# A graph layer on one core: the first batch's inputs come and are split by chunks, its scores are finished earlier, its delta is turned by TensorE, and the groups are ordered by weight

## The chip, the cores and the metric

The kernel runs on one core of a Trainium2 chip. The metric is the time of one execution on the device in microseconds (us). Several executions are timed and their median is taken; one more execution was recorded by the profiler, and its trace is what this text reads. The engines are TensorE (PE), VectorE (DVE), ScalarE (ACT), GpSimd (POOL) and SyncE (SP), which here does nothing but issue DMAs. Each engine works through its own instructions in order.

## The reference

For each of 32 batches, with h = x[b] of 256 rows and 384 features:

```python
u = h @ h.T / sqrt(384)
p = softmax(u, axis=-1)
delta = p * adjacency
attn = delta / (delta.sum(2) + 1e-10)
h_left, h_self, h_right = (h @ W.T + b for the three weights and biases)
ctx = upper(attn) @ h_left + diag(attn) * h_self + lower(attn) @ h_right
o = relu(layernorm(ctx, eps=1e-12) * gamma + beta)
out = layernorm(x + o, eps=1e-5)
```

All of it is float32.

## The kernel before

A float32 operand is split into two halves, `hi` (rounded by ScalarE's copy to fp32r) and `lo` (the rest, a subtraction on VectorE), and each product is three TensorE passes: hi·hi, hi·lo, lo·hi. The pieces of a batch are:

- **Scores.** x comes a second time with features before rows (`x_t`), three chunks of 128 features by 256 rows. For batch 0 all 18 matmuls of three passes are done (`scores`, by way of `product`, L361). For the others the lo·hi term is computed once (`cross`, 6 matmuls, L388), turned on VectorE in 32x32 blocks (`turn_cross`, L597), sent to DRAM and read back so that the blocks change places (`store_cross`, `load_cross`), while TensorE adds hi·hi to it (`squares`, 6 matmuls, L397). `finish_scores` (L613) adds the turned part and takes the row minimum.
- **Softmax and delta.** `exps` (ACT L463, two instructions), `deltas` (DVE L621), then delta has to be turned: `turn` (DVE L629), `store_turned` (SP L277, one DMA to DRAM), `load_turned` (SP L283, four DMAs back), `split_delta` (ACT L489, DVE L647), and `triangles` (POOL L854).
- **Projections.** Six groups g of (weight, row tile), nine matmuls of 384 columns each (`project`, L361), in four PSUM banks that take turns. Each bank is first filled with the bias by `seed_proj` (ACT L478). The first four are split by `split_proj` (ACT L482, DVE L641). Groups 4 and 5 (the self weight) need a bank that an earlier group has left.
- **Context.** `seed_ctx` (ACT L497), then `attend` for two row tiles, nine matmuls each (L420), then the two norms on DVE, POOL and ACT, a batch later.

There is no planner: the order on each engine is written out by hand, for batch b and its neighbours. Four places matter here.

TensorE in batch b: `squares(b+1)`, groups 0 to 4, `cross(b+2)`, group 5, `attend` 0 and 1. In batch 0 `cross(1)` comes after group 3 and `squares(1)` after group 4.

ScalarE in batch b >= 1: `split_delta(b)` first, `split_proj(b, 0)`, `normalise(b-1)`, `split_proj(b, 1)`, `exps(b+1)`, and only then `seed_proj(b, 4)`.

VectorE in batch b >= 1: norm work of b-1, `split_delta(b)`, `norm_shift(b-1)`, `split_proj(b, 0)`, `finish_scores(b+1)`, `split_proj(b, 1)`, `deltas(b+1)`, `turn(b+1)`, and so on.

SyncE in batch 0, after the start: `load_xt(3)`, the loads of x and adj of batch 2, `store_turned(1)`, `store_cross(2)`, `load_turned(1)`, `load_cross(2)`. Every store waits for its VectorE transpose, every load back waits for its store, and whatever stands behind waits too.

The start is written apart. All inputs are requested by SyncE in one go: x_t of batch 0, left weight, three biases, adj 0, x_t 1, right weight, self weight, gamma, beta, x_t 2, x 0, x 1, adj 1, each as one DMA. Then `store_turned(0)` with `load_turned(0)`, then `store_cross(1)` with `load_cross(1)`. ScalarE waits for all three biases (`biases_loaded`) ahead of its first seed; VectorE has this order, in which `finish_scores` stands behind the low halves of two weights:

```python
split_xt(first)
split_weight(LEFT)
split_weight(RIGHT)
finish_scores(first)
```

TensorE opens its banks with six matmuls of zeros (L426) and then does 16 warm-up transposes of the identity (L430) ahead of the scores of batch 0.

Of the kernel before, what the change touches and what calls it, by code (L numbers as in the profile page):

```python
# [73 lines left out]
def gnn_resnorm(nc, x, x_t, adj, wt_left, b_left, wt_self, b_self, wt_right, b_right, gamma, beta, out):  # L74
# [6 lines left out]
    WARM_UP = 16  # L81
    LARGEST = 3.0e38

    GROUPS = [(LEFT, 0), (RIGHT, 0), (LEFT, 1), (RIGHT, 1), (SELF, 0), (SELF, 1)]
# [13 lines left out]
        [(MASK_LEFT, 0, 0), (MASK_RIGHT, 0, 1), (FULL, 1, 2)],  # L98
        [(FULL, 2, 1), (MASK_LEFT, 1, 2), (MASK_RIGHT, 1, 3)],
    ]  # L100

    with ExitStack() as ctx:
# [75 lines left out]
        w_loaded = [sem(f"w_loaded{w}") for w in range(3)]  # L178
        biases_loaded = sem("biases_loaded")
# [16 lines left out]
        dt_loaded = sem("dt_loaded")  # L196
        cross_ready = sem("cross_ready")
# [69 lines left out]
        def _(sp):  # L267
# [7 lines left out]
            def store_turned(at):  # L275
                sp.wait_ge(turned_ready, at.n(1, 1))
                sp.dma_start(dt_dram[:], turned[:]).then_inc(turned_stored, 16)  # L277

            def load_turned(at):

                sp.wait_ge(turned_stored, at.n(16, 16))
                for q in range(Q):
                    sp.dma_start(dt_raw[q * R:(q + 1) * R].rearrange("p a k r -> p a (k r)"), dt_rows[q]).then_inc(dt_loaded, 16)  # L283
# [13 lines left out]
            sp.dma_start(xt_sb[0][:], xt_rows[0]).then_inc(xt_loaded[0], 16)  # L297
            biases = (b_left, b_right, b_self)
            for w, wt in ((LEFT, wt_left), (RIGHT, wt_right), (SELF, wt_self)):
                sp.dma_start(w_raw[w][:], wt.rearrange("(c p) e -> p c e", p=P)).then_inc(w_loaded[w], 16)  # L300
                if w == LEFT:
                    for v in range(3):
                        sp.dma_start(bias[v][:, 0:H], biases[v].partition_broadcast(P)).then_inc(biases_loaded, 16)  # L303
                    sp.dma_start(adj_sb[0][:], adj_rows[0]).then_inc(adj_loaded[0], 16)
                    load_xt(1, 1)
# [15 lines left out]
            def one(at):  # L321
# [3 lines left out]
                if third.exists(BATCHES):  # L325
                    if at.plus(-1).exists(BATCHES):
                        sp.wait_ge(xt_lo_ready, at.n(1, 0))
                    load_xt(third.n(1), third.slot(UNROLL))
                if ahead.exists(BATCHES):
# [6 lines left out]
                if ahead.exists(BATCHES):  # L336
# [3 lines left out]
                if ahead.exists(BATCHES):  # L340
                    load_cross(ahead)
# [15 lines left out]
        def _(pe):  # L357
            def product(to, pairs, seeded):
                passes = [(s[i], m[j]) for s, m in pairs for i, j in ((0, 0), (0, 1), (1, 0))]
                for k, (stationary, moving) in enumerate(passes):  # L360
                    mm = nc.tensor.matmul(to, stationary, moving, start=(k == 0 and not seeded),  # L361
                                          stop=(k == len(passes) - 1), skip_group_check=seeded)
                return mm

# [4 lines left out]
            def scores(at):  # L369
                pe.wait_ge(xt_lo_ready, at.n(1, 1))  # L370
                for t in range(T):
                    mm = product(ps_scores[at.slot(2)][:, t, :],
                                 [(xt(at, c, t * P, (t + 1) * P), [keys(m) for m in xt(at, c, 0, L)]) for c in range(C)], False)
                mm.then_inc(scores_ready, 1)
# [5 lines left out]
            def cross(at):  # L380
                pe.wait_ge(xt_lo_ready, at.n(1, 1))
# [19 lines left out]
            def project(at, g):  # L401
                w, t = GROUPS[g]
                if at.b == 0 and t == 0:
                    pe.wait_ge(w_lo_ready[w], 1)
                pe.wait_ge(proj_seeded, at.n(NG, g + 1))
                product(ps_proj[bank(at, g)][:, 0:H],
                        [(xt(at, c, t * P, (t + 1) * P), (w_hi[w][:, c, :], w_lo[w][:, c, :])) for c in range(C)],
                        True).then_inc(proj_ready, 1)
# [23 lines left out]
            scores(first)  # L432

            def one(at):
# [20 lines left out]
        def _(act):  # L455
# [3 lines left out]

            def exps(at):  # L460
# [6 lines left out]
            def seed_proj(at, g):  # L467
                w, _ = GROUPS[g]
                if g >= PBANKS:
# [4 lines left out]
                elif at.b != 0:  # L474
# [9 lines left out]
            def split_delta(at):  # L484
                act.wait_ge(dt_loaded, at.n(64, 64))
                if at.b != 0:

                    act.wait_ge(ctx_ready, at.n(T, 0))
                nc.scalar.activation(dt_full[:, 0, :, :].rearrange("p k (a r) -> p k a r", a=Q),  # L489
                                     dt_raw[:].rearrange("p a k r -> p k a r"), ACT.Copy).then_inc(dt_hi_ready, 1)  # L490

            def seed_ctx(at, t):

                act.wait_ge(proj_ready, at.n(NG, order(at).index(NSPLIT + t) + 1))
                if t == 0:
                    act.wait_ge(diag_ready, at.n(T, T))
                nc.scalar.activation(ps_ctx[:, t, 0:HE], ps_proj[bank(at, NSPLIT + t)][:, 0:HE], ACT.Copy,  # L497
# [20 lines left out]
            split_xt(first)  # L518
            act.wait_ge(banks_opened, 1)
            act.wait_ge(ones_ready, 1)  # L520
            act.wait_ge(w_loaded[LEFT], 16)
# [394 lines left out]
```

## Time and profile before

| | |
|---|---|
| median of three executions | 488.22 us (486.7, 488.4, 488.22) |
| profiled execution, its own time | 486.24 us |
| its span, first to last instruction | 484.5 us |
| TensorE matmuls busy | 460.5 us, 95% of the span |
| VectorE, ScalarE, GpSimd busy | 357.5, 324.7, 223.5 us |
| mean granted TensorE clock | 0.977 |

The span is shorter than the execution's own time by what lies around the first and the last instruction (486.24 less 484.5 is 1.7 us). Busy time says how long an engine had an instruction in work; what ended an engine's idle time is told by the wait and chain views. The granted clock is 1.0 for 2.4 GHz and 0.5 for 1.2 GHz. Times of day below are in us from the start of the span.

### The profile page before, as it was taken

The page shows a single profiled execution, that of the slowest core. Times are in us where ns is not written, and L with a number is a line of the kernel's source. Part 1 is how long each engine was busy: PE and PEld are TensorE (multiplying, and loading weights), DVE is VectorE, ACT ScalarE, POOL GpSimd, SP SyncE. Part 2 cuts the span into 40 slices and gives each one's busy share as a digit, 9 for nine tenths or more (in the row PEclk, how much of TensorE's full clock was granted, in tenths as well). Part 3 has the DMA queues.
Part 4 walks back from the last instruction along what each step waited for, and adds up shares of the span by engine and source line. Part 5 has one row for each costly group of instructions (what it writes and reads, how often), then busy time and mean ns, then how long its engine had stood idle before and what let it go on. Part 6 is the DMA issues. An engine that isn't in the chain of part 4 may idle for free.

```text
span 484.5 us, 9588 instructions
## 1 busy us (share of the span) xinstructions
PE 460.5 (95%) x2716; PEld 457.6 (94%) x2716; DVE 357.5 (74%) x1077; ACT 324.7 (67%) x706; POOL 223.5 (46%) x295
## 2 busy tenths in 40 slices
PE   6749999999999999999999999999999999999992
PEld 6739999999999999999999999999999999999982
DVE  2536887877788887777887877777887777886756
ACT  4425577767766876676677766766776677677752
POOL 0212345554444455544445554445455544455552
PEclk9597999999999999999999999999999999999997
DMA  8635355556645555656445556654555656454211
GB/s 238 233 105 190 104 183 177 188 182 192 196 136 183 178 185 174 200 184 197 145 158 187 184 178 193 196 178 147 168 184 177 196 184 200 148 169 141 88 71 65
DMA packets 86226, 82.16 MB, mean 170 GB/s; under 512 B 7232, under 2 KB 78144, under 8 KB 86208
## 3 DMA queue, kind: packets, MB, share of 16 engines
q1 hardware_dynamic: 86208, 81.95, 53.2%
q8 instruction: 8, 0.13, 0.1%
q14 instruction: 10, 0.08, 0.1%
HBM read 52.82 MB, written 29.10 MB: 169 GB/s over the span
## 4 chain that ended last, share of the span: by engine, by line
PE 88%; DMA 3%; DVE 3%; issue 2%; POOL 2%; ACT 1%; SPq 1%; POOLq 0%; DVEq 0%
PE ps_proj L361 58%; PE ps_ctx L420 21%; PE ps_scores L397 5%; PE ps_scores L388 4%; DMA w_raw<-in_L_gnn_W_right 2%; POOL rstd L860 1%; POOL shifted L868 0%; DMA dt_raw<-dt_dram 0%; DMA dt_dram<-turned 0%; POOL scaled L864 0%; DVE stats L652 0%; DVE w_lo L699 0%; SPq L303 0%; SPq L283 0%; ACT w_hi L528 0%
## 5 line engine op out<-in xcount | busy, mean ns | idle before, releaser
L361 PE MATMUL ps_proj<-w_hi,xt_hi 128*128 128x384 f32 x576 | 195.4, 339 | 7.8 <-ACT ps_proj L478 4.8
L361 PE MATMUL ps_proj<-w_lo,xt_hi 128*128 128x384 f32 x576 | 195.0, 339 | 0.0
L361 PE MATMUL ps_proj<-w_hi,xt_lo 128*128 128x384 f32 x576 | 195.0, 338 | 0.0
L860 POOL TENSOR_TENSOR rstd<-var_eps,minus_half 128x4 f32<-128x4 f32 x32 | 43.0, 1345 | 195.0 <-DVE var_eps L671 192.5
L361 PEld LDWEIGHTS ps_proj<-w_hi,xt_hi 128*128 128x128 f32 x576 | 109.5, 190 | 9.0 <-issue 4.8
L361 PEld LDWEIGHTS ps_proj<-w_lo,xt_hi 128*128 128x128 f32 x576 | 109.3, 190 | 0.0
L361 PEld LDWEIGHTS ps_proj<-w_hi,xt_lo 128*128 128x128 f32 x576 | 109.2, 190 | 0.0
L482 ACT ACTIVATE proj_hi<-ps_proj 128x384 fp32r<-128x384 f32 x128 | 63.4, 495 | 53.9 <-PE ps_proj L361 53.7
L478 ACT ACTIVATE ps_proj<-bias 128x384 f32<-128x384 f32 (+1 forms) x192 | 92.6, 496 | 3.3 <-DMA bias<-in_L_gnn_b_self 3.2
L641 DVE TENSOR_TENSOR proj_lo<-ps_proj,proj_hi 128x384 fp32r<-128x384 f32 x128 | 68.3, 548 | 14.0 <-ACT proj_hi L482 13.8
L864 POOL TENSOR_TENSOR scaled<-normed,gamma_sb 128x384 f32<-128x384 f32 x62 | 63.2, 1019 | 31.9 <-ACT normed L503 31.9
L868 POOL TENSOR_TENSOR shifted<-scaled,beta_sb 128x384 f32<-128x384 f32 x62 | 68.7, 1108 | 2.4
L497 ACT ACTIVATE ps_ctx<-ps_proj,diag 128x386 f32<-128x386 f32 x64 | 35.6, 557 | 37.9 <-PE ps_proj L361 34.7
L652 DVE BATCH_NORM_STATS2 stats<-ps_ctx 128x6 f32<-128x384 f32 x64 | 36.2, 565 | 32.5 <-PE ps_ctx L420 29.9
L420 PE MATMUL ps_ctx<-proj_hi,dt_left 128*128 128x386 f32 x128 | 44.2, 346 | 5.3 <-issue 5.3
L489 ACT ACTIVATE dt_full<-dt_raw 128x512 fp32r<-128x512 f32 x32 | 20.2, 632 | 36.8 <-DMA dt_raw<-dt_dram 27.1
L420 PE MATMUL ps_ctx<-proj_hi,dt_right 128*128 128x386 f32 x128 | 43.8, 342 | 0.0
L503 ACT ACTIVATE normed<-ps_ctx,shift,rstd 128x384 f32<-128x384 f32 x62 | 38.3, 668 | 6.5 <-DVE shift L678 6.5
L513 ACT ACTIVATE out_sb<-y_sb,shift,rstd 128x384 f32<-128x384 f32 x62 | 40.1, 696 | 0.1
L420 PE MATMUL ps_ctx<-proj_hi,dt_full 128*128 128x386 f32 x128 | 39.1, 345 | 0.6 <-ACT ps_ctx L497 0.6
L685 DVE SCALAR_TENSOR_TENSOR y_sb<-shifted,x_sb 128x384 f32<-128x384 f32 x62 | 36.7, 592 | 1.9 <-POOL shifted L868 1.9
L690 DVE BATCH_NORM_STATS2 stats<-y_sb 128x6 f32<-128x384 f32 x64 | 35.9, 561 | 2.2
(80 smaller groups left out, 656.8 us busy)
## 6 DMA issues: line engine op xcount, KB each, us to landing
xt_sb<-in_x_t SPq DMA_DIRECT2D x32, 384.0 KB, 3.7
x_sb<-in_x SPq DMA_DIRECT2D x32, 384.0 KB, 4.3
out_dram<-out_sb SPq DMA_DIRECT2D x31, 384.0 KB, 2.8
adj_sb<-in_adj SPq DMA_DIRECT2D x32, 256.0 KB, 4.4
dt_dram<-turned SPq DMA_DIRECT2D x32, 256.0 KB, 2.0
dt_raw<-dt_dram SPq DMA_DIRECT2D x128, 64.0 KB, 2.0
cross_dram<-cross_turned SPq DMA_DIRECT2D x31, 256.0 KB, 2.0
cross_raw<-cross_dram SPq DMA_DIRECT2D x124, 64.0 KB, 2.0
```

Source lines behind the costliest of these rows:

```text
L361: mm = nc.tensor.matmul(to, stationary, moving, start=(k == 0 and not seeded), stop=(k == len(passes) - 1), skip_group_check=seeded)
L420: mm = nc.tensor.matmul(ps_ctx[:, t, 0:HE], s, m, start=False, stop=True, skip_group_check=True)
L478: nc.scalar.activation(ps_proj[bank(at, g)][:, 0:to], bias[w][:, 0:to], ACT.Copy).then_inc(proj_seeded, 1)
L482: nc.scalar.activation(proj_hi[:, g, 0:H], ps_proj[bank(at, g)][:, 0:H], ACT.Copy).then_inc(proj_hi_ready, 1)
L503: nc.scalar.activation(normed[:, t, :], ps_ctx[:, t, 0:H], ACT.Identity, bias=shift[at.slot(2)][:, t:t + 1], scale=rstd[at.slot(2)][:, t:t ...
L513: nc.scalar.activation(out_sb[at.slot(2)][:, t, :], y_sb[at.slot(2)][:, t, :], ACT.Identity, bias=shift[nxt][:, T + t:T + t + 1], scale=rs ...
L641: nc.vector.tensor_tensor(proj_lo[:, g, 0:H], ps_proj[bank(at, g)][:, 0:H], proj_hi[:, g, 0:H].bitcast(F32), ALU.subtract).then_inc(proj_l ...
L652: nc.vector.bn_stats(stats1[:, t, :], ps_ctx[:, t, 0:H]).then_inc(stats1_ready, 1)
L685: nc.vector.scalar_tensor_tensor(y_sb[at.slot(2)][:, t, :], shifted[:, t, :], 0.0, x_sb[at.slot(UNROLL)][:, t, :], ALU.max, ALU.add).then_ ...
L860: nc.gpsimd.tensor_tensor(rstd[at.slot(2)][:], var_eps[:], minus_half[:], ALU.pow).then_inc(rstd_ready, 1)
L864: nc.gpsimd.tensor_tensor(scaled[:, t, :], normed[:, t, :], gamma_sb[:], ALU.mult).then_inc(scaled_ready[t], 1)
L868: nc.gpsimd.tensor_tensor(shifted[:, t, :], scaled[:, t, :], beta_sb[:], ALU.add).then_inc(shifted_ready[t], 1)
```

## The change

It touches the start, batch 0 and the order of the groups:

- The x_t of batch 0 comes in three DMAs and each weight in three, one per chunk of 128 features, each with a semaphore. The splits of them (ACT, DVE, and POOL for the self weight) are by chunk. Each bias has its own semaphore and is requested behind its weight. adj 1 is requested ahead of gamma and beta, x 0 behind `store_cross(1)`, and x 1 in batch 0.
- The groups are ordered left 0, left 1, right 0, right 1, self 0, self 1, in all batches; `attend` takes the same products by their new numbers.
- Warm-up transposes: 4, not 16. The scores of batch 0 are done chunk by chunk. `finish_scores(0)` stands behind one chunk of one weight's low half.
- The delta of batch 0 is turned by four TensorE transposes into the PSUM bank of context tile 1 (`first_turn`, behind group 1), and split from there. Its trip to DRAM and back is gone. The bank is opened again by a matmul of zeros (`open_context`).
- In batch 0 TensorE does `squares(1)` and `cross(2)` behind group 5. On ScalarE and VectorE the order of batch 0 is written anew. On SyncE `store_cross(2)`, `load_cross(2)` and x 1 come ahead of the loads of batch 2 and of `store_turned(1)`.

The core of the diff:

```diff
-    WARM_UP = 16
+    WARM_UP = 4
-    GROUPS = [(LEFT, 0), (RIGHT, 0), (LEFT, 1), (RIGHT, 1), (SELF, 0), (SELF, 1)]
+    GROUPS = [(LEFT, 0), (LEFT, 1), (RIGHT, 0), (RIGHT, 1), (SELF, 0), (SELF, 1)]
...
         def _(sp):
...
+            for c in range(C):
+                sp.dma_start(xt_sb[0][:, c, :], xt_rows[0][:, c, :]).then_inc(first_xt_loaded[c], 16)
+            load_weight(LEFT)
+            load_bias(LEFT)
+            sp.dma_start(adj_sb[0][:], adj_rows[0]).then_inc(adj_loaded[0], 16)
+            load_weight(RIGHT)
+            load_bias(RIGHT)
+            load_xt(1, 1)
+            load_weight(SELF)
+            load_bias(SELF)
+            load_xt(2, 2)
+            sp.dma_start(adj_sb[1][:], adj_rows[1]).then_inc(adj_loaded[1], 16)
             for to, vector in ((gamma_sb, gamma), (beta_sb, beta)):
                 sp.dma_start(to[:], vector.partition_broadcast(P)).then_inc(vectors_loaded, 16)
-            load_xt(2, 2)
+            first = Batch(0, 0)
+            store_cross(first.plus(1))
             sp.dma_start(x_sb[0][:], x_rows[0]).then_inc(x_loaded[0], 16)
-            load(1, 1)
-            first = Batch(0, 0)
-            store_turned(first)
-            load_turned(first)
-            store_cross(first.plus(1))
             load_cross(first.plus(1))
...
                     load_xt(third.n(1), third.slot(UNROLL))
+                if at.b == 0:
+                    store_cross(ahead)
+                    load_cross(ahead)
+                    sp.dma_start(x_sb[1][:], x_rows[1]).then_inc(x_loaded[1], 16)
                 if ahead.exists(BATCHES):
...
                     load(ahead.n(1), ahead.slot(UNROLL))
                 if nxt.exists(BATCHES):
                     store_turned(nxt)
-                if ahead.exists(BATCHES):
+                if ahead.exists(BATCHES) and at.b != 0:
                     store_cross(ahead)
                 if nxt.exists(BATCHES):
                     load_turned(nxt)
...
         def _(pe):
...
+            def first_turn(at):
+
+                pe.wait_ge(delta_ready, T)
+                for t in range(T):
+                    for h in range(T):
+                        k = T * t + h
+                        mm = nc.tensor.transpose(ps_ctx[:, 1, k * P:(k + 1) * P], delta[:, t, h * P:(h + 1) * P], ident[:])
+                mm.then_inc(first_dt_ready, 1)
+
+            def open_context(at):
+                pe.wait_ge(dt_lo_ready, 1)
+                nc.tensor.matmul(ps_ctx[:, 1, 0:HE], zeros[:, 0:P], zeros[:], start=True, stop=True).then_inc(ctx_opened, 1)
...
+                    if at.b == 0 and g == 1:
+                        first_turn(at)
                     if at.b == 0 and g == 3:
                         cross(nxt)
-                    if at.b == 0 and g == 4:
-                        squares(nxt)
-                    if g == 4 and ahead.exists(BATCHES):
+                    if g == 4 and at.b != 0 and ahead.exists(BATCHES):
                         cross(ahead)
+                if at.b == 0:
+                    open_context(at)
+                    squares(nxt)
+                    cross(ahead)
...
         def _(act):
...
+            split_first_xt()
+            for c in range(C):
+                split_weight(LEFT, c)
             act.wait_ge(banks_opened, 1)
             act.wait_ge(ones_ready, 1)
...
+            for g in range(2):
                 seed_proj(first, g)
...
             exps(first)
+            for c in range(C):
+                split_weight(RIGHT, c)
+            for g in range(2, PBANKS):
+                seed_proj(first, g)
+            for g in range(2):
+                split_proj(first, g)
             split_xt(first.plus(1))
+            split_weight(SELF, 0)
+            seed_proj(first, 4)
+            for c in range(1, C):
+                split_weight(SELF, c)
+            seed_proj(first, 5)
+            split_delta(first)
             split_xt(first.plus(2))
+            for g in range(2, NSPLIT):
+                split_proj(first, g)
+            for t in range(T):
+                seed_ctx(first, t)
+            for g in range(2):
+                seed_proj(first.plus(1), g)
+            exps(first.plus(1))
+            for g in range(2, PBANKS):
+                seed_proj(first.plus(1), g)
+            split_xt(first.plus(3))
...
         def _(dve):
...
-            split_weight(LEFT)
-            split_weight(RIGHT)
+            split_weight(LEFT, 0)
             finish_scores(first)
+            for c in range(1, C):
+                split_weight(LEFT, c)
             dve.wait_ge(moments_ready, 1)
             deltas(first)
-            turn(first)
+            for c in range(C):
+                split_weight(RIGHT, c)
+            for g in range(2):
+                split_proj(first, g)
+            split_xt(first.plus(1))
             dve.wait_ge(ident_ready, 1)
             diagonal(first)
-            split_xt(first.plus(1))
+            turn_cross(first.plus(1))
+            split_delta(first)
             split_xt(first.plus(2))
+            for g in range(2, NSPLIT):
+                split_proj(first, g)
+            finish_scores(first.plus(1))
+            turn_cross(first.plus(2))
+            deltas(first.plus(1))
+            turn(first.plus(1))
+            diagonal(first.plus(1))
+            split_xt(first.plus(3))
```

## Rows read from the trace of the kernel before

**Rows 1.** The page: busy us, share of the span and instructions by engine.
```profile
PE 460.5 (95%) x2716; PEld 457.6 (94%) x2716; DVE 357.5 (74%) x1077; ACT 324.7 (67%) x706; POOL 223.5 (46%) x295
```

**Rows 2.** Windows: start:end, length, busy (instructions) per engine, clock, DMA share, GB/s.
```profile
6.00:7.00 1.00, 1.00 (x10) 0.95 (x9) 0.00 (x0) 0.97 (x1) 0.00 (x0) 1.00 0.98 153
...
8.46:10.82 2.36, 0.00 (x0) 0.03 (x1) 0.00 (x0) 0.64 (x2) 0.00 (x0) 1.00 1.02 331
...
16.22:22.05 5.83, 5.83 (x18) 5.83 (x19) 4.61 (x14) 3.01 (x8) 2.65 (x1) 0.50 0.55 190
...
32.37:36.98 4.61, 0.00 (x0) 0.03 (x1) 1.31 (x7) 1.56 (x6) 0.00 (x0) 0.87 0.81 252
36.98:42.78 5.80, 5.80 (x18) 5.80 (x19) 3.46 (x9) 2.76 (x6) 0.00 (x0) 0.51 0.41 138
...
49.86:56.90 7.04, 7.04 (x44) 7.04 (x44) 6.41 (x16) 4.02 (x8) 2.08 (x3) 1.00 0.32 107
56.90:70.86 13.96, 13.96 (x85) 13.96 (x85) 11.00 (x33) 10.04 (x22) 6.64 (x9) 1.00 0.50 159
```

**Rows 3.** Chain of waits, batch 2 on: start, length, what ran.
```profile
65.58 0.71 PE ps_scores L388 x6
66.29 1.56 PE ps_proj L361 x9
67.85 3.17 PE ps_ctx L420 x18
```

**Rows 4.** Timeline of all engines, the start: start, length, engine, line, instruction.
```profile
3.50 2.68 PE L430 MATMUL ps_scores<-ident 128*128 128x128 f32 x16
...
4.16 0.84 ACT L458 ACTIVATE xt_hi<-xt_sb 128x768 fp32r<-128x768 f32 x1 [2.06 <-DMA xt_sb<-in_x_t]
...
7.00 1.36 DVE L699 TENSOR_TENSOR w_lo<-w_raw,w_hi 128x1152 fp32r<-128x1152 f32 x1 [1.00 <-ACT w_hi L522]
...
10.18 1.73 ACT L478 ACTIVATE ps_proj<-bias 128x384 f32<-128x384 f32 x4 [3.21 <-DMA bias<-in_L_gnn_b_self]
...
13.61 1.16 ACT L528 ACTIVATE w_hi<-w_raw 128x1152 fp32r<-128x1152 f32 x1 [1.70 <-DMA w_raw<-in_L_gnn_W_right]
...
16.09 0.43 DVE L613 CUSTOM_DVE_ANT_0 ps_scores<-ps_scores,zeros 128x256 f32<-128x256 f32 x1
```

**Rows 5.** DMA issues of the first 45 us: size, us from issue to landing.
```profile
bias<-in_L_gnn_b_left SPq DMA_DIRECT2D x1, 192.0 KB, 5.3
```

**Rows 6.** Timeline of SyncE: when DMAs were issued, and how long issuing took.
```profile
1.83 0.48 SPq L303 DMA_DIRECT2D bias<-in_L_gnn_b_left  x1
...
29.08 0.34 SPq L288 DMA_DIRECT2D cross_dram<-cross_turned  x1
31.13 1.73 SPq L294 DMA_DIRECT2D cross_raw<-cross_dram  x4
...
33.38 0.49 SPq L269 DMA_DIRECT2D x_sb<-in_x  x1
33.91 0.47 SPq L270 DMA_DIRECT2D adj_sb<-in_adj  x1
38.07 0.34 SPq L277 DMA_DIRECT2D dt_dram<-turned  x1
...
40.72 1.75 SPq L283 DMA_DIRECT2D dt_raw<-dt_dram  x4
```

**Rows 7.** Timeline of all engines, batch 1.
```profile
34.52 0.43 DVE L613 CUSTOM_DVE_ANT_1 ps_scores<-ps_scores,cross_raw 128x256 f32<-128x256 f32 x1 [5.46 <-issue]
...
44.24 0.64 ACT L489 ACTIVATE dt_full<-dt_raw 128x512 fp32r<-128x512 f32 x1 [4.50 <-DMA dt_raw<-dt_dram]
...
48.17 0.50 ACT L478 ACTIVATE ps_proj<-bias 128x386 f32<-128x386 f32 x1
...
49.86 0.34 PE L361 MATMUL ps_proj<-w_hi,xt_hi 128*128 128x384 f32 x1
```

**Rows 8.** The page's DMA issues: KB each, median us from issue to landing.
```profile
adj_sb<-in_adj SPq DMA_DIRECT2D x32, 256.0 KB, 4.4
```

More of the change, by code:

```diff
@@ L177, in gnn_resnorm @@
         adj_loaded = [sem(f"adj_loaded{i}") for i in range(UNROLL)]
[L178 to L179 removed]
+        first_xt_loaded = [sem(f"first_xt_loaded{c}") for c in range(C - 1)] + [xt_loaded[0]]
+        w_loaded = [[sem(f"w_loaded{w}_{c}") for c in range(C)] for w in range(3)]
+        bias_loaded = [sem(f"bias_loaded{w}") for w in range(3)]
         vectors_loaded = sem("vectors_loaded")
@@ L339, in one @@
                     load_turned(nxt)
-                if ahead.exists(BATCHES):
+                if ahead.exists(BATCHES) and at.b != 0:
                     load_cross(ahead)
@@ L357, in _ @@
         def _(pe):
[L358 to L363, printed above, removed]
             def xt(at, c, a, b):
@@ L402, in project @@
                 w, t = GROUPS[g]
-                if at.b == 0 and t == 0:
-                    pe.wait_ge(w_lo_ready[w], 1)
                 pe.wait_ge(proj_seeded, at.n(NG, g + 1))
-                product(ps_proj[bank(at, g)][:, 0:H],
-                        [(xt(at, c, t * P, (t + 1) * P), (w_hi[w][:, c, :], w_lo[w][:, c, :])) for c in range(C)],
-                        True).then_inc(proj_ready, 1)
+                for c in range(C):
+                    if at.b == 0 and t == 0:
+                        pe.wait_ge(w_lo_ready[w], c + 1)
+                    hi, lo = xt(at, c, t * P, (t + 1) * P)
+                    for stationary, moving in ((hi, w_hi), (hi, w_lo), (lo, w_hi)):
+                        mm = nc.tensor.matmul(ps_proj[bank(at, g)][:, 0:H], stationary, moving[w][:, c, :], start=False, stop=True,
+                                              skip_group_check=True)
+                mm.then_inc(proj_ready, 1)
             def attend(at, t):
@@ L431, in _ @@
             first = Batch(0, 0)
-            scores(first)
+            first_scores(first)
             def one(at):
@@ L468, in seed_proj @@
                 w, _ = GROUPS[g]
+                if at.b == 0 and g == PBANKS:
+                    act.wait_ge(bias_loaded[w], 16)
                 if g >= PBANKS:
@@ L536, in one @@
                 if at.b == 0:
-                    split_proj(at, 0)
-                    split_delta(at)
-                else:
-                    split_delta(at)
-                    split_proj(at, 0)
-                if before.exists(BATCHES):
-                    normalise(before)
+                    return
+                split_delta(at)
+                split_proj(at, 0)
+                normalise(before)
                 split_proj(at, 1)
-                if at.b != 0 and nxt.exists(BATCHES):
+                if nxt.exists(BATCHES):
                     exps(nxt)
@@ L645, in split_delta @@
                 dve.wait_ge(dt_hi_ready, at.n(1, 1))
+                if at.b == 0:
+                    lo, hi = (dt_full[:, half, :, :].rearrange("p k e -> p (k e)") for half in (1, 0))
+                    nc.vector.tensor_tensor(lo, ps_ctx[:, 1, :], hi.bitcast(F32), ALU.subtract).then_inc(dt_lo_ready, 1)
+                    return
                 lo, hi = (dt_full[:, half, :, :].rearrange("p k (a r) -> p k a r", a=Q) for half in (1, 0))
@@ L725, in one @@
                 nxt, ahead, third = at.plus(1), at.plus(2), at.plus(3)
-                if before.exists(BATCHES):
-                    context_stats(before, 1)
-                    norm_variances(before)
-                    norm_var_eps(before, before.n(T, T), second.n(T, T) if second.exists(BATCHES) else None)
-                    split_delta(at)
-                    norm_shift(before)
-                split_proj(at, 0)
-                if at.b == 0:
-                    split_delta(at)
-                    for g in range(1, NSPLIT):
-                        split_proj(at, g)
-                    turn_cross(nxt)
+                if at.b == 0:
+                    context_stats(at, 0)
+                    return
+                context_stats(before, 1)
+                norm_variances(before)
+                norm_var_eps(before, before.n(T, T), second.n(T, T) if second.exists(BATCHES) else None)
+                split_delta(at)
+                norm_shift(before)
+                split_proj(at, 0)
                 if nxt.exists(BATCHES):
                     finish_scores(nxt)
-                if at.b != 0:
-                    split_proj(at, 1)
+                split_proj(at, 1)
                 if nxt.exists(BATCHES):
```

125 lines of the change are left out of this document (66 added, 59 removed).

## The prediction

> **What bounds the kernel now.** I read the busy times first, then the chain of waits over the span, then windows, then timelines around each TensorE idle time. TensorE's matmuls are busy 95% of the span [rows 1]. The windows show where the other 5% lies: a whole batch, 56.90 to 70.86, has TensorE busy 13.96 of 13.96 us at clock 1.00 [rows 2], and the chain from then on is TensorE alone, piece after piece [rows 3], up to a tail of norms at the very end that the change leaves alone. So the time is: when TensorE's last idle time ends and its clock is back, plus a constant. The change adds no work to batches 1 to 31; the new order of groups uses the same banks, the same matmuls and the same waits, and its cost there is nothing, because all low halves are ready well before `attend`.
>
> Before, TensorE waits at 8.46 to 10.82 for the seeds, which wait for the last of three biases [rows 2, 4]; then for the right weight, which lands at 13.61; then for delta's trip through DRAM. `finish_scores(0)` starts at 16.09 [rows 4] though the scores end near 8.5, because it stands behind two weights. The longest wait, 32.37 to 36.98, ends when `seed_ctx(0)` comes behind `exps(1)`, which waited for the cross part that came back at 34.52 [rows 2, 7]. After it 18 matmuls take 5.80 us at clock 0.51 [rows 2], where 18 take 3.17 at full clock [rows 3]. Group 4 of batch 1 starts at 49.86 [rows 7], and nothing stops TensorE after that. That is the mark: where does group 4 of batch 1 start afterwards?
>
> **The start.** An x_t load of 384 KB gives ScalarE its split at 4.16 [rows 4]. By chunks I put the first at 3.2, the others 0.5 apart (a SyncE issue takes 0.43 to 0.49 [rows 6]). A ScalarE split of 256 columns is 0.38 and one of 384 is 0.49 (768 take 0.84, 1152 take 1.16), a VectorE one of 384 is 0.5 to 0.55 (1152 take 1.36) [rows 4]; splitting by chunks costs about 0.3 more per weight on each, beside DMA waits. Chunk low halves are ready at 4.1, 4.6, 5.1. TensorE has opened its banks at 3.5; the 16 transposes took 2.68, some at half rate and some at full [rows 4]; four take 0.85, so the scores start at 4.35 and, first at 1.2 and then at 2.4 GHz, end at 6.8 (8.5 before). The left bias landed at 1.83+5.3=7.1 [rows 5, 6] behind the same bytes as now, so I take 6.9: two seeds till 7.8, `finish_scores` 6.9 to 7.8, the left low halves till 8.9. Groups 0 and 1, 1.56 each [rows 3], run from 7.45 with small gaps to 11.0; `exps` ends at 8.9, `deltas` at 9.8, so `first_turn` (four transposes, 0.5) finds delta ready. The right weight lands by 9.9 and the right bias at about 10.5 (the DMA engines move the same bytes, ordered otherwise), seeds 2 and 3 end at 11.4, groups 2 and 3 at 14.6. ScalarE has split groups 0 and 1 and x_t 1 by 13.2, VectorE follows at 14.15, so `cross(1)` runs 14.6 to 15.4 and `turn_cross(1)`, 0.7, ends at **16.2**. Before it ended at 29.08, where its store is issued [rows 6]: 12.9 earlier.
>
> The rest of batch 0 is not late: self low halves on GpSimd (2.65 in all by [rows 2]) let group 4 end at 17.7 and group 5 at 19.3; delta's halves are ready at 17.6; gamma and beta, which GpSimd waits for ahead of `triangles`, land near 18. The extra opening matmul (0.2), `squares(1)`, `cross(2)` (0.7 each) and 3.17 of `attend` end at 24.1. `squares(2)` and groups 0 to 3 of batch 1 (0.71 and 6.25) end at 31.05. If TensorE were all, group 4 would start here, 18.8 us earlier than before.
>
> **The wait that takes the place.** Group 4 needs `seed_proj(1, 4)`, which stands on ScalarE behind `split_delta(1)`, which waits for delta 1 from DRAM. So follow SyncE, in its order. `store_cross(1)` at 16.2; from store to `finish_scores` was 29.08 to 34.52 [rows 6, 7], 5.4, so 21.7 (x 0, issued between, has passed before the four loads want the DMA engines). `finish_scores(1)` 0.87, `turn_cross(2)` 0.7: 23.3. Now SyncE, in the new order, does `store_cross(2)`, its 2.05 of landing and four issues of 1.75 [rows 6]: 27.15. Then x 1, x 2, adj 2 at 0.53 each [rows 6]: 28.8. Only then comes `store_turned(1)`, though delta 1 is turned at about 25.5. Three loads of 384, 384 and 256 KB are queued ahead of its 256 KB. A store with nothing ahead lands after 2.05 [rows 6]; adj, the last of such a triple, lands 4.4 after its issue [rows 8], and the store is issued 0.5 later and moves another 0.7: 4.6. I take 4.3, near the loaded one: 33.1. The four loads back take 3.4 to 3.5 till ScalarE's split (40.72 to 44.24 [rows 6, 7]): **36.5**. From there to the seed of group 4 is 44.24 to 48.17 [rows 7], plus 0.5 for the seed: group 4 starts at **40.9**. Nothing of that piece gets shorter: the 1.3 us of norm shift, `normalise` and `exps(2)` in it wait for VectorE's half of delta 1 as before.
>
> TensorE thus idles from 31.05 to 40.9, 9.8 us. After 4.61 idle the trace shows 18 matmuls at 5.80 instead of 3.17, and after the idle times of the start 18 more took 5.83 [rows 2]: a restart at 1.2 GHz costs 2.6. It is paid once before too (36.98), but ahead of the mark, so it counts here in full. Everything later is then covered: delta 2 follows `cross(3)` by the same steps and is needed only at group 4 of batch 2, a batch's work later.
>
> **Sum.** 49.86 - (40.9 + 2.6) = 6.4 us less. Against the profiled execution, 486.24 (span 484.5 and 1.7 around it), that is 479.9; against the median, 488.22, which is 2.0 above it, 481.8. I say 481.0, between the two. About 0.5% (2.4 us) is what a measurement of this kernel can tell from no change.
>
> **Small loads.** The change makes nine 192 KB loads and three of 128 KB out of four large ones. The trace has loads of 64 KB four in a row, issued over 1.75 and all in by 3.5 [rows 6, 7], so their latencies overlap; my sum gives a chunk its share of the bytes. The Trainium skill (DMA: Bandwidth & Descriptors, Measured (HBM→SBUF, 128 partitions, SWDGE, issued from GpSimd)) tells to batch DMAs to 1 MiB or more for 75% of peak, which speaks against this change. That section measured another issue path; no row here has a weight in chunks, so it is kept as the third case below.
>
> **The rivals.**
>
> *The write is not held up by the loads.* `store_turned(1)` lands 2.05 after issue, not 4.3. For it: stores before landed so. Against: none of those had a megabyte just ahead. Group 4 starts at 38.6: 2.3 better, 478.7.
>
> *Small loads are slow.* For it: while biases (192 KB) were coming, the DMA engines were busy 0.98 and moved 153 GB/s, against 331 two us later [rows 2]. Against: a bias is one row read for all 128 partitions, a weight chunk isn't. If the six chunks of left and right weight ran at 153, each would take 1.3 instead of 0.6; 0.7 by six is 4.2 ahead of the right bias, less about 0.7 of slack there: 3.5 later at 16.2, and all of it at the mark. 484.5. The skill's rule would lead here.
>
> *The clock stays at 1.2 GHz through batch 0.* The end on the other side. For it: TensorE now does only four transposes, idles around 7 and 8, and after 8.46 to 10.82 idle the clock was down at 16.22 to 22.05 [rows 2]. Price: 18 score matmuls at 0.21 end at 8.2; 36 projections at 0.32 instead of 0.173 cost 5.3, the rest of the chain (gaps, transposes, `cross`) 0.3 more: 16.2 becomes 23.2, group 4 starts at 47.9 and with the restart at 50.5 in effect, 0.7 later than before: 488.9 against the median of before. It decides from 6.4 us of loss ahead of 16.2 on. Against: the idle pieces are under 1 us each, and before the clock came back after 5.8 us of unbroken work.
>
> *No stall.* TensorE goes on at 31.05 and all 18.8 us stay: 468.6. It would take `store_turned(1)` at 25.5, ahead of what stands before it in SyncE's order; the trace shows SyncE in order throughout.
>
> **The numbers.** Forecast 0.60; write not held up 0.18; small loads slow 0.12; clock stays down 0.06; no stall 0.02; the rest something that I don't see. The range: at the low end the free write, one us off the start, a restart that costs one us less and runs like the profiled one, 476; at the high end the slow loads and a us more, 485.5. The forecast's own range is 479 to 483. Faster by over 0.5% means under 485.8: nearly all of the first three and the stall-free, 0.90. Within 0.5%: the worse part of the slow loads, and most of the clock case, 0.07. Slower by over 0.5%: 0.03.
>
> **What would show it.** `turn_cross(1)` ending near 16; SyncE issuing `store_turned(1)` near 29, 3 us behind its VectorE transpose; `split_delta(1)` near 36.5 as the wait that ends last; TensorE idle 9 to 10 us ahead of group 4 of batch 1, clock 0.50 behind it; batches of 13.96 after that. The prediction is wrong if the scores end far from 6.8, if the store of delta 1 lands within 2.5 of its issue, if TensorE has a gap over 2 us in batch 0, or if a later batch has one at all.

## The result, and the profile after

| | before | changed |
|---|---|---|
| median | 486.91 us (8 runs, 485.65 to 488.42) | 483.76 us (8 runs, 482.46 to 485.92) |
| ratio, 95% interval | | 0.993, 0.991 to 0.9949 |
| profiled execution, its span | 486.24, 484.5 us | 482.74, 481.0 us |

The kernel became 0.7% faster: 3.1 us by the medians, 3.5 us between the two profiled executions. The forecast was 481.0, in 476 to 485.5. The eight executions put the kernel before at 486.91; the three that the forecast had to go by, at 488.22.

The page of the changed kernel and its windows (start:end, length, busy time and instructions per engine, clock, DMA share, GB/s), cut at the places where TensorE stops and starts, answer to [rows 1, 2]:

```profile
PE 455.7 (95%) x2709; PEld 453.1 (94%) x2709; DVE 360.1 (75%) x1082; ACT 325.5 (68%) x714; POOL 224.6 (47%) x297
```

```profile
6.85:9.77 2.92, 0.00 (x1) 0.00 (x1) 1.84 (x7) 1.07 (x3) 0.00 (x0) 1.00 1.00 305
9.77:17.45 7.68, 7.68 (x47) 7.65 (x48) 5.97 (x11) 7.52 (x20) 2.26 (x2) 1.00 0.94 321
17.45:26.00 8.55, 8.25 (x51) 7.62 (x49) 4.66 (x13) 4.06 (x11) 3.16 (x6) 1.00 0.52 155
26.00:33.30 7.30, 7.30 (x42) 6.97 (x42) 4.20 (x15) 1.96 (x5) 1.03 (x1) 1.00 0.53 147
33.30:44.21 10.91, 0.00 (x1) 0.00 (x0) 2.92 (x10) 3.97 (x11) 2.15 (x5) 0.60 0.60 190
44.21:53.58 9.37, 9.37 (x42) 9.37 (x43) 6.88 (x18) 4.68 (x10) 3.43 (x4) 0.74 0.30 93
53.58:67.55 13.97, 13.97 (x86) 13.97 (x86) 11.06 (x33) 9.99 (x22) 6.85 (x9) 1.00 0.45 150
```

Read them from the top. Once group 0 starts at 9.77, TensorE works nearly without a gap to 33.3, where four groups of batch 1 are done; before, that point was 49.86 [rows 7], so this is 16.6 us earlier. Then it stands still for 10.9 us. The piece from group 4 to the end of batch 1, 7.04 us before [rows 2], takes 9.37, since the clock comes back only within it. A batch is 13.97 us again, as before. So 16.6 us were gained, 10.9 lost in one wait and 2.3 in the restart: 3.3 of 16.6 remain, and that is the gain. The first window shows a smaller idle time of 2.92 us in batch 0, ahead of group 0.

What the stall waits for is in the chain of waits of the changed kernel (start, length, what ran):

```profile
25.93 2.02 DMA cross_dram<-cross_turned
27.97 0.31 SPq L298
...
29.75 0.43 SPq L345
...
30.23 0.47 SPq L273
...
30.74 0.47 SPq L274
...
31.25 5.01 DMA dt_dram<-turned
36.28 0.33 SPq L287
...
37.60 2.16 DMA dt_raw<-dt_dram
39.78 0.64 ACT dt_full L540
```

L298 is the cross load, L345 x 1, L273 and L274 are x 2 and adj 2, L281's store is the 5.01. Delta 1 has been turned at 28.0. The timeline gives the marks at both ends of the stall (answers to [rows 4, 7]):

```profile
3.49 1.06 PE L461 MATMUL ps_scores<-ident 128*128 128x128 f32 x4
...
6.90 0.43 DVE L679 CUSTOM_DVE_ANT_0 ps_scores<-ps_scores,zeros 128x256 f32<-128x256 f32 x1 [0.97 <-issue]
...
9.22 0.91 ACT L526 ACTIVATE ps_proj<-bias 128x384 f32<-128x384 f32 x2 [0.97 <-DMA bias<-in_L_gnn_b_left]
...
17.59 0.70 DVE L663 STREAM_TRANSPOSE cross_turned<-ps_scores 128x512 f32<-128x512 f32 x1
...
39.78 0.63 ACT L540 ACTIVATE dt_full<-dt_raw 128x512 fp32r<-128x512 f32 x1 [11.83 <-DMA dt_raw<-dt_dram]
...
43.65 0.52 ACT L526 ACTIVATE ps_proj<-bias 128x386 f32<-128x386 f32 x1
...
44.21 0.69 PE L437 MATMUL ps_proj<-w_hi,xt_hi 128*128 128x384 f32 x1 [10.91 <-ACT ps_proj L526]
```

The last line names ScalarE's seed as the releaser. ScalarE was itself idle for 11.83 us ahead of `split_delta(1)`; its own wait is for the four loads of delta 1. The engine that is named is only the last link.

### The profile page after: what moved, and what is told of

It reads as the page before. It is cut to its first block, busy times and chain, and to the rows that moved or that the text cites. A ratio compares the mean times of both kernels' runs of the same rounds, so it can differ in the third digit from the quotient of the medians.

```text
span 481.0 us, 9617 instructions
## 1 busy us (share of the span) xinstructions
PE 455.7 (95%) x2709; PEld 453.1 (94%) x2709; DVE 360.1 (75%) x1082; ACT 325.5 (68%) x714; POOL 224.6 (47%) x297
## 4 chain that ended last, share of the span: by engine, by line
PE 87%; DMA 3%; POOL 2%; ACT 2%; DVE 2%; issue 2%; SPq 1%; POOLq 0%; DVEq 0%; ACTq 0%
PE ps_proj L437 58%; PE ps_ctx L451 20%; PE ps_scores L425 4%; PE ps_scores L416 4%; DMA bias<-in_L_gnn_b_left 1%; DMA dt_dram<-turned 1%; POOL w_lo L926 1%; POOL rstd L940 1%; POOL shifted L948 0%; DMA dt_raw<-dt_dram 0%; ACT ps_proj L526 0%; DMA cross_dram<-cross_turned 0%; POOL scaled L944 0%; ACT normed L556 0%; ACT ps_scores L507 0%
## 5 line engine op out<-in xcount | busy, mean ns | idle before, releaser
L707 DVE TENSOR_TENSOR proj_lo<-ps_proj,proj_hi 128x384 fp32r<-128x384 f32 x128 | 69.3, 547 | 15.2 <-ACT proj_hi L530 14.7
L451 PE MATMUL ps_ctx<-proj_hi,dt_full 128*128 128x386 f32 x128 | 38.1, 337 | 0.6 <-ACT ps_ctx L550 0.6
```

The source lines that it names most:

```text
L451: mm = nc.tensor.matmul(ps_ctx[:, t, 0:HE], s, m, start=False, stop=True, skip_group_check=True)
L707: nc.vector.tensor_tensor(proj_lo[:, g, 0:H], ps_proj[bank(at, g)][:, 0:H], proj_hi[:, g, 0:H].bitcast(F32), ALU.subtract).then_inc(proj_l ...
```

## The experiments

Each ratio is to the kernel before on the same chip; that kernel's median was 486.91, 486.12 and 485.74 us in the three sets of runs.

**1. Delta 1 first on SyncE.** In batch 0:

```diff
                 if at.b == 0:
                     store_cross(ahead)
+                    store_turned(nxt)
+                    load_turned(nxt)
                     load_cross(ahead)
                     sp.dma_start(x_sb[1][:], x_rows[1]).then_inc(x_loaded[1], 16)
+                    load(ahead.n(1), ahead.slot(UNROLL))
+                    return
```

> The changed kernel, with SyncE's order in batch 0 altered: store and load of delta 1 right behind the cross store of batch 2, then the cross load, x 1, x 2, adj 2. Theory (the stall is delta 1 queued behind other DMAs of SyncE): delta 1's store is issued as soon as it is turned, near 28.0 instead of 31.25, lands 2 later, its four loads are in near 33.5 to 34.0 instead of 39.8, group 4 of batch 1 starts near 38.2 instead of 44.2, and the whole is 5 to 6 us faster than the changed kernel, about 478. Rival (a late load holds it: the start decides, or batch 1's ScalarE chain has another wait of the same length): under 1 us faster. Rival (x 1, x 2 and adj 2, now later, hold up the norms or the scores of a later batch): a new TensorE gap over 1 us in batch 2 or 3.

Measured: 477.35 us, ratio 0.9821 (0.9792 to 0.985). Its chain and its windows around the stall:

```profile
28.55 2.00 DMA dt_dram<-turned
30.57 0.32 SPq L287
...
31.89 2.22 DMA dt_raw<-dt_dram
34.13 0.64 ACT dt_full L544
```

```profile
33.80:38.55 4.75, 0.04 (x1) 0.00 (x0) 2.58 (x9) 3.97 (x11) 2.15 (x5) 1.00 0.79 254
38.55:47.21 8.66, 8.66 (x42) 8.66 (x43) 6.91 (x18) 4.68 (x10) 3.25 (x4) 0.80 0.62 210
47.21:61.17 13.96, 13.96 (x85) 13.96 (x85) 10.87 (x33) 9.90 (x22) 6.66 (x9) 1.00 0.49 159
```

The store lands in 2.00 instead of 5.01, delta 1 is split at 34.13 instead of 39.78, group 4 starts at 38.55 instead of 44.21, and the next batches have no gap. The same computation and the same DMAs, in another order on one queue, are worth 6.4 us by the medians and 5.3 by the ratios, more than the whole change gave. So 6.2 of the 10.9 us of the stall are shown to come from SyncE's order. The other 4.75 remain with delta 1 first: group 4 still waits for `split_delta(1)`, whose input is on its way from 28.55 to 34.13. No run makes that trip shorter.

**2. The loads between store and load of delta 1.** As 1, but the cross load, then delta 1's store, then x 1, x 2, adj 2, then delta 1's loads.

> The changed kernel with delta 1's store ahead of x 1, x 2 and adj 2, but its load back behind them; the cross load stays ahead of all. Theory (the DMA engines take what SyncE queued in order, a megabyte ahead costs 2.5 to 3 us): the store, nothing ahead of it, lands 2.0 to 2.2 after its issue instead of 5.0, and the four loads back, now behind the megabyte, are in 4.5 to 5 us after their first issue instead of 3.5; delta 1 is there near 36.5, 3 us earlier than in the changed kernel. Rival (the store was slow for another reason, for instance writes wait for reads in flight): it still takes over 4 us.

Measured: 480.18 us, 0.9869 (0.9848 to 0.989). From its chain:

```profile
29.39 2.47 DMA dt_dram<-turned
31.88 0.33 SPq L287
...
33.19 4.06 DMA dt_raw<-dt_dram
37.27 0.64 ACT dt_full L544
```

The last load back took 4.06 us from its issue instead of 2.16: what stands behind the megabyte pays, store or load. The store, now just ahead of the megabyte, pays little (2.47). The rival, that this store is slow by itself, falls. Group 4 started at 41.70, between the changed kernel and experiment 1.

**3. Left bias first.**

```diff
+            load_bias(LEFT)
             for c in range(C):
                 sp.dma_start(xt_sb[0][:, c, :], xt_rows[0][:, c, :]).then_inc(first_xt_loaded[c], 16)
             load_weight(LEFT)
-            load_bias(LEFT)
```

> The changed kernel with the left bias requested ahead of x_t 0 instead of behind the left weight. Theory (group 0 waits for the left bias, and every us at turn_cross(1) is a us at the end): group 0 starts when the left weight's low halves are there, near 9.0 to 9.3 instead of 9.77 since x_t and the weight come 0.5 to 1 later, and the whole is 0.5 to 1 us faster. If the low rate of the DMA engines between 5 and 8 us is the bias's own (one row read for 128 partitions), that dip moves to 2 to 4 us; if it stays at 5 to 8, it is not the bias's. Rival (group 0 is bound by something else): no difference at turn_cross(1).

Measured: 483.64 us, 0.9926 (0.991 to 0.9942): no gain. The bias was there 3.2 us after its issue at 0.82, but x_t came later, and the 18 score matmuls took 4.0 us (5.34 to 9.35) where the changed kernel needs 2.5. They start 0.21 apart, where most of the changed kernel's start 0.12 apart; I read this as 1.2 GHz, though the windows list the granted clock as 1.00 here, as they do for the start of every run. `finish_scores(0)` began at 9.59 instead of 6.90. Group 0 did its first chunk at 9.35 and then waited till 10.93 for the left low halves. I had counted with the byte shares alone and not with the clock. In this kernel's windows the DMA engines moved 149 GB/s from 2 to 3 us, but 257 from 6 to 7, where the changed kernel moved 143: the dip goes with the bias. The other nine traces with the changed kernel's start have 109 to 192 from 6 to 7.

**4. Whole loads.**

```diff
-            for c in range(C):
-                sp.dma_start(xt_sb[0][:, c, :], xt_rows[0][:, c, :]).then_inc(first_xt_loaded[c], 16)
+            sp.dma_start(xt_sb[0][:], xt_rows[0]).then_inc(xt_loaded[0], 16)
...
-                for c in range(C):
-                    sp.dma_start(w_raw[w][:, c, :], w_rows[w][:, c, :]).then_inc(w_loaded[w][c], 16)
+                sp.dma_start(w_raw[w][:], w_rows[w]).then_inc(w_loaded[w][0], 16)
```

ScalarE's waits are on the one semaphore of each tile.

> The changed kernel with x_t 0 and the three weights requested whole, one DMA each, while all splits stay by chunks. Theory (the bytes of the start come later because chunks are small and issued one by one): scores end 1 us later than 6.7, but the left bias is in near 7.3 instead of 9.1, group 0 starts near 9.3, and the whole is the same or up to 1 us faster. Rival (chunks pay): the scores, which end at 7.8, and the left low halves behind them make group 0 start after 10, and the whole is 0.5 to 1 us slower.

Measured: 482.7 us, 0.9913 (0.9895 to 0.993). Seeds start at 8.73 instead of 9.22, `finish_scores(0)` at 7.49 instead of 6.90, group 0 at 9.27 instead of 9.77. Chunks therefore bring nothing at the end; the intervals overlap, so that they cost something isn't shown. But the left bias landed 6.8 us after its issue at 1.83, at 8.6 and not at 7.3: in this trace it is late with whole loads around it too.

**5. Sixteen warm-ups**, run twice: `WARM_UP = 16` in the changed kernel.

> The changed kernel with 16 warm-up transposes again. Theory (the start is set by the left bias and the seeds behind it, so 12 transposes less are worth nothing at the end): scores end near 8.2 instead of 6.7, finish_scores 1.4 later, but exps stands behind the seeds that end at 10.1 and group 0 starts at 9.8 to 10.0; the whole is within 0.3 us of the changed kernel. Rival (the warm-ups are part of the gain): 1 to 1.5 us slower.

Measured: 481.63 us, 0.9897 (0.9866 to 0.9928), faster than the changed kernel, which neither side had expected. So both ran again, side by side:

> The changed kernel itself, beside the next ones on one chip, so that their warm-ups are compared directly. Both theories: 0.991 to 0.995 of the kernel before.

> The changed kernel with 16 warm-up transposes, once more. The first run of this came out at 0.9897 of the kernel before, where the changed kernel was at 0.993, though I had expected no difference. Theory (4 warm-ups leave TensorE idle some 3 us ahead of group 0, in which the clock can fall or fail to rise, while 16 leave 1.3): 1 to 2 us faster than the changed kernel on the same chip, and the clock never at 0.5 between 6 and 30 us. Rival (the first run was scatter): within 0.5 us.

Measured: the changed kernel 484.2 us (11 runs, 482.08 to 486.82), 0.9957 (0.9933 to 0.9981); with 16 warm-ups 482.12 us (6 runs, 480.99 to 483.14), 0.9903 (0.9872 to 0.9934). The gain came out both times, 1.6 us by the ratios the first time and 2.1 by the medians the second: the removal of 12 transposes, meant to let the scores start sooner, makes the kernel slower. The two intervals of the second time just touch, but of its 66 pairs of one execution with each kernel, the one with 16 warm-ups is the faster in 58. Why is less sure. The profiled executions of the two started group 4 at 44.20 and 44.52, but they can't explain the medians: the one of the changed kernel is the fastest of its eleven (482.08), the other the slowest of its six (483.14).

The traces show two ways in which it can happen. The first is the clock. In the windows of experiment 7 below, which has 4 warm-ups too, TensorE had idled for 2.05 us ahead of group 0, and the clock was at 1.2 GHz for group 0 and beyond:

```profile
7.30:9.35 2.05, 0.00 (x1) 0.01 (x1) 1.75 (x7) 1.07 (x3) 0.00 (x0) 0.95 1.03 351
9.35:12.60 3.25, 3.25 (x10) 3.25 (x11) 1.82 (x5) 3.25 (x10) 0.00 (x0) 0.50 1.08 373
```

Ten matmuls in 3.25 us are 1.5 us lost. Experiment 8, with 4 warm-ups and 1.79 us of idle time there, shows the same fall a little later. In the profiled executions of the changed kernel and its variants with 16 warm-ups (four) the clock did not fall there, nor in experiment 1, which had idled for 2.92. So the length of the idle time alone does not decide it. The mean clocks of the runs fit this way: of the changed kernel's eleven, the slowest (486.82) has the lowest, 0.974, and four others are under 0.980, while the six with 16 warm-ups have 0.981 to 0.984.

The second is the cross part. From the issue of `store_cross(1)` to the start of `finish_scores(1)` the four traces with 16 warm-ups (these two, experiments 9 and 10) took 5.46 to 5.81 us, and their SyncE issued the four cross loads in 1.75 or 1.76. The seven with 4 warm-ups and the loads in chunks took 6.06 to 7.56, and the issue 2.42 to 3.21. Experiment 4, with 4 warm-ups and whole loads, has 1.75 and 6.07. Nothing in the traces ties this to the transposes. That either costs 2 us in the median is argued, not shown.

**6. The order of the groups alone**, in the kernel before (`GROUPS` and `ATTEND` of the diff, nothing else).

> The kernel before with the new order of groups and nothing else. Theory (batches 1 to 31 are TensorE alone and the order costs or gives nothing there): a batch stays at 13.96 us; in batch 0, groups 0 and 1 run ahead of the right weight, which lets TensorE work in 12.9 to 16.2 where it idled, worth up to 1.6 us ahead of delta's trip, but the longest wait (for the cross part, by way of SyncE) is not made shorter: under 1 us either way. Rival (the order of groups is where the gain comes from): 2 us or more faster.

Measured: 485.98 us, 0.9996 (0.9965 to 1.0027). No difference, as expected; within 1.5 us the part that touches all 32 batches is worth nothing by itself. What the order does inside the changed kernel, where it lets groups 0 and 1 run on the left weight alone, was not taken out and measured.

**7. x 0 later**, on top of 1: x 0 goes from behind `store_cross(1)` to behind the cross load of batch 2.

> The kernel with delta 1 first (e1_delta_first) and x 0 moved from between the cross store and cross load of batch 1 to behind the cross load of batch 2. Theory (every us on the chain cross part, finish_scores(1), delta 1 is a us at group 4 of batch 1, until the stall is gone): the four cross loads are issued in 1.75 instead of 2.96 us and land 1 to 1.3 earlier, group 4 starts near 37.3 instead of 38.55, the whole is about 1 us faster than with delta 1 first, near 476.3. Rival (x 0, now later, is waited for by the residual of batch 0, or the stall has another tail): no gain.

Measured: 477.53 us, 0.9823 (0.9751 to 0.9896). No gain beside 1. With x 0 gone, issuing the four cross loads took 2.43 us, against 2.96 in experiment 1 and 2.42 in the changed kernel, and `finish_scores(1)` started 4.0 us after the first of them, against 4.6 and 4.0. The 1.75 that I expected did not come, and the four traces with 16 warm-ups have it with x 0 in its old place, so x 0 is not what makes the issue long. The clock's fall shown above also sits in the profiled execution, so the small edit could not have been read from it alone.

**8. Self weight's low halves on VectorE**, on top of 7: GpSimd's loop is taken out and `split_weight(SELF, c)` put around `diagonal(first)`.

> As e7_x0_late, with the low halves of the self weight made by VectorE instead of GpSimd. In the changed kernel the two diagonal instructions of batch 0 took 1.1 us each while GpSimd worked on these, and 0.25 to 0.28 in batch 1 with GpSimd idle. Theory (the two engines hold each other up): with GpSimd idle they take 0.25 to 0.3; turn_cross(1) was waiting for cross(1), not for them, so the end gains under 0.3 us. Rival (the instructions are slow in batch 0 for another reason, such as reading the identity for the first time): they stay at 1.1.

Measured: 478.26 us, 0.9818 (0.9755 to 0.988): same at the end. The diagonal instructions in the timeline of the changed kernel, GpSimd at work beside them:

```profile
15.53 1.11 DVE L701 SCALAR_TENSOR_TENSOR on_diag<-delta,ident 128x128 f32<-128x128 f32 x1
16.57 0.08 DVE L701 DVE_READ_ACCUMULATOR on_diag<-delta,ident 128x1 f32 x1
16.57 1.09 DVE L701 SCALAR_TENSOR_TENSOR on_diag<-delta,ident 128x128 f32<-128x128 f32 x1
```

and in this one, where GpSimd does nothing till 20.41:

```profile
17.27 0.28 DVE L705 SCALAR_TENSOR_TENSOR on_diag<-delta,ident 128x128 f32<-128x128 f32 x1
17.49 0.08 DVE L705 DVE_READ_ACCUMULATOR on_diag<-delta,ident 128x1 f32 x1
17.49 0.28 DVE L705 SCALAR_TENSOR_TENSOR on_diag<-delta,ident 128x128 f32<-128x128 f32 x1
```

The rival, that they are slow in batch 0 for another reason, falls. These instructions are off the path that sets the time.

**9. Delta 1 first and 16 warm-ups.**

> Delta 1 first (as e1_delta_first) and 16 warm-ups. Theory (both gains stand on the same chain and add up): 5.5 to 6.5 us faster than the changed kernel by the order, 1 more by the warm-ups, so about 0.979 of the kernel before. Rival (the second gain is taken by the stall): as e1_delta_first, 0.982.

Measured: 475.73 us (474.67 to 476.26), 0.9776 (0.9745 to 0.9807). Against 1 that is about 1.6 us by the medians and 2.2 by the ratios, and the intervals overlap; it agrees with both gains adding up.

**10. Kept busy in the stall**, on top of 9:

```diff
                     project(at, g)
+                    if at.b == 1 and g == 3:
+                        pe.wait_ge(delta_ready, 2 * T)
+                        for _ in range(32):
+                            nc.tensor.transpose(ps_scores[1][:, 0, 0:P], ident[:], ident[:])
```

> As e11_first_warm16, with 32 transposes of the identity put behind group 3 of batch 1, where TensorE waits 4.7 us for group 4's seed; they write a score bank whose delta is done and that is overwritten next. Theory (the restart at 1.2 GHz behind the stall costs 1.7 to 2.6 us): they run in about 3.7 us at 2.4 GHz, the clock stays at 1.0 behind them, group 4 starts when it did and the whole is 1.5 to 2.5 us faster than e11_first_warm16. Rival (transposes do not keep the clock up): the clock falls as before, same time.

Measured: 474.61 us (474.24 to 474.7), 0.9752 (0.9723 to 0.9782). Its timeline and windows:

```profile
33.31 3.66 PE L482 MATMUL ps_scores<-ident 128*128 128x128 f32 x32
37.98 0.44 PE L441 MATMUL ps_proj<-w_hi,xt_hi 128*128 128x384 f32 x1 [1.02 <-ACT ps_proj L534]
```

```profile
33.00:39.00 6.00, 4.98 (x41) 4.71 (x40) 2.66 (x9) 4.99 (x13) 3.17 (x6) 1.00 0.81 243
39.00:45.00 6.00, 6.00 (x37) 5.85 (x36) 5.61 (x15) 3.69 (x8) 2.25 (x3) 1.00 0.71 244
37.98:45.18 7.20, 7.20 (x42) 7.05 (x43) 5.79 (x15) 4.71 (x10) 3.27 (x4) 1.00 0.73 251
```

The same piece, group 4 to the end of batch 1, in experiment 9, which has no transposes in the stall:

```profile
37.46:46.12 8.66, 8.66 (x43) 8.66 (x43) 6.92 (x18) 4.67 (x10) 3.22 (x4) 0.80 0.70 225
```

The clock stays at 1.00, and the piece takes 7.20 instead of 8.66 (7.04 at full clock). Of these 1.5 us, 0.5 is lost because group 4 starts at 37.98 and not at 37.46. The gain by the medians is 1.1 us, less than the 1.5 to 2.5 expected. The restart itself does not follow the length of the stall: behind 4.5 to 4.7 us it cost 1.6 in experiments 1 and 9 and 2.2 in 7 and 8; behind 10.9 it cost 2.3 in the changed kernel, but 1.65 in its repeat behind 10.75. What differs is how long the clock stays at 0.50 once group 4 runs, some 4.9 us in the changed kernel and 3.4 in experiment 1. The six runs of this version lie within 0.5 us, the narrowest of all. This version beats both kernels: 2.5% under the one before and, by the ratios, about 2% under the changed one.

## Why the prediction was right, and where its sizes were off

The kernel became faster, by the mechanism that was forecast, and the time lies in the range; the gain was about half of the 6.4 us, because the left bias, the cross part's trip and delta 1's store were taken as too quick. The measured 483.76 lies outside the forecast's own 479 to 483. The wider range held it with some luck: its upper end was set by the slow loads, which did not come.

*The mark.* "Nothing stops TensorE after that" held: batches of 13.97, the order of groups alone worth nothing that experiment 6 could measure.

*The start.* Scores ended at 6.8, as forecast; `finish_scores(0)` began at 6.90. The step that was off is "the left bias landed at 1.83+5.3=7.1 behind the same bytes as now, so I take 6.9". It landed at 3.61+5.5=9.1, group 0 started at 9.77 and not 7.45, and `turn_cross(1)` ended at 18.3 and not 16.2: 2.1 us. The same bytes ahead were not the same time: in the ten traces that issue this bias at 3.61, or 3.62, behind the chunks, it took 4.7 to 6.2 us and landed at 8.3 to 9.8, never near 6.9. In experiment 4 it was issued at 1.83 behind the same two loads as in the kernel before, with other DMAs behind it, and landed at 8.6 instead of 7.1. That is one trace against one, and a spread of 1.5 us is also what the ten show among themselves, so what makes it late is open.

TensorE thus had an idle time of 2.92 us in batch 0, ahead of group 0. The prediction had named a gap over 2 us there as a sign that it is wrong, and against the clock case it had set that "the idle pieces are under 1 us each". On this point its picture of the start was wrong. In the changed kernel's two traces the clock did not fall for it; in those of experiments 7 and 8 it did. ScalarE's pieces, taken at 0.38 and 0.49 us, took 0.42 to 0.53.

*The wait that takes the place.* Everything in this part came as written, in its order: SyncE's cross store, cross load, x 1, x 2, adj 2, then delta 1; ScalarE's `split_delta(1)` as the wait that ends last. From `turn_cross(1)` to the issue of delta 1's store 13.0 us were measured, 12.6 forecast (the cross part's trip, from store to `finish_scores(1)`, took 6.15 instead of 5.4, and the steps behind it a little less than forecast); the store 5.0 against 4.3 (I had bounded it at 4.6); loads to split 3.5 against 3.4 to 3.5; split to group 4 4.43, as forecast. SyncE issued delta 1's store at 31.25, 3.25 behind its transpose. The store took over 2.5, so this sign of being wrong did not come. The late start was passed on at its full size: 2.1+0.4+0.7+0.1 is 3.3, and group 4 came at 44.2 and not at 40.9.

*The restart* cost 2.3 against 2.6, and 1.65 in the repeat. The Trainium skill (TensorE: Matmul & The Clock Gate, Part 4: PE-mode transpose) states that the clock's upper level does not engage for transpose-mode, since a transpose does not count as busy time in the same way; its figures there are for bf16. Experiment 10 speaks against it, as far as this kernel goes: 32 float32 transposes alone filled 3.66 of 4.68 us, and the clock of the windows behind them is 1.00, where it was 0.80 without them. It shows that they kept the clock up, not that they can raise it, and the trace lists them as matmuls without their mode.

*The sum* was then 49.86 - (44.21 + 2.33) = 3.3 instead of 6.4, beside 3.5 measured between the profiled executions. For the repeat, 49.86 - (44.20 + 1.65) = 4.0, beside 4.2.

*The rivals.* The write not held up by the loads: refuted by 5.01, and experiment 1 shows what it is without them. Small loads slow: by the medians experiment 4 leaves 1.1 us for it, which the intervals of the two don't separate from nothing, and not the 3.5 of the case. The rule that speaks for large DMAs (the Trainium skill, DMA: Bandwidth & Descriptors, Measured (HBM→SBUF, 128 partitions, SWDGE, issued from GpSimd)) would lead to whole loads, but no measurable gain came from following it here. The clock at 1.2 GHz through the start: not in the changed kernel's two profiled executions, but a low clock there does occur, for 3 us in experiment 7 and as long in 8, and in experiment 3 the scores took 4.0 us instead of 2.5. The expectation of experiment 5, that the 12 warm-ups are worth nothing at the end, was wrong by 2 us. No stall: refuted.

## What to carry to other kernels

When a stage is pulled ahead, follow each queue that feeds the next stage, in issue order: here 16.6 us were won on TensorE and 13.2 given back, 5 to 6 of them because one queue, SyncE's, kept a megabyte of early loads and the cross load ahead of a 256 KB round trip that had become the critical one. Order a DMA queue by when each transfer is waited for, not by when its source is free. And where TensorE must wait, count the restart of its clock too, and hold work that only keeps it busy (warm-ups, transposes into a bank that is overwritten) against that cost before removing it.

## What the runs showed of the hardware that I had not expected

- GpSimd's work held VectorE up. A 128x128 scalar_tensor_tensor on VectorE took 1.11 and 1.09 us while GpSimd made low halves, and 0.28 each with GpSimd idle (experiment 8). Not every instruction suffers: the 32x32 transpose right behind, with GpSimd still at work, took 0.70, as long as without it.
- One load's time to landing varies from execution to execution: the left bias, issued at the same time in the same queue, took 4.7 to 6.2 us in ten traces.
- While a bias, one row to 128 partitions, was coming, the DMA engines moved 143 GB/s from 6 to 7 us in the changed kernel, and the dip moved with the bias in experiment 3.
- The slow clock behind a stall of 4.5 to 4.7 us cost 1.6 to 2.2 us, that behind one of 10.8 or 10.9 cost 1.65 and 2.3, and that behind one of 4.7 us filled with transposes 0.2.
